# Both score products of a chunk as one group of 128 columns, and another order of L, mask and u

## What is computed

```python
attn = jnp.where(mask_incl, 0.0, -(kbc @ jnp.swapaxes(kc, -1, -2)))
for i in range(1, chunk):
    row = attn[..., i, :]
    upd = jnp.einsum('bhnj,bhnjk->bhnk', row, attn[..., :i])
    attn = attn.at[..., i, :i].add(upd)
attn = attn + jnp.eye(chunk, dtype=attn.dtype)
u = attn @ vc
w = attn @ kbc
def step(S, xs):
    q_i, k_i, u_i, w_i = xs
    attn_local = jnp.where(mask_strict, 0.0, q_i @ jnp.swapaxes(k_i, -1, -2))
    u_new = u_i - w_i @ S
    o_i = q_i @ S + attn_local @ u_new
    S = S + jnp.swapaxes(k_i, -1, -2) @ u_new
    return (S, o_i)
```

## Time and profile before

| | |
|---|---|
| median of 3 runs | 1094.88 us (1090.1 to 1096.59) |
| profiled execution | 1092.34 us, span 1090.6 us |
| busy over the span | PE 798.0 us, PE weight loads 495.7, DVE 743.3, ACT 454.5, POOL 201.5 |
| mean granted clock of TensorE | 0.856 |
| front stage | until about 622 us; rounds 0 to 15 start on DVE from 153.1 to 603.7 us |
| 390 to 450 us (60 us) | PE busy 57.74, DVE 56.02, ACT 33.08 |

### The profile page before, as it was taken

How to read it: one execution, slowest core, us unless ns; L and a number is a source line. 1 busy time by engine, 2 the same in 40 slices (tenths; PEclk the granted TensorE clock), 3 DMA queues, 4 the chain that set the end, 5 groups by cost and what they waited for, 6 DMA issues and landing times. The chain is left out here.

```text
span 1090.6 us, 40949 instructions
## 1 busy us (share of the span) xinstructions
PE 798.0 (73%) x18289; PEld 495.7 (45%) x18289; DVE 743.3 (68%) x1612; ACT 454.5 (42%) x864; POOL 201.5 (18%) x223
## 2 busy tenths in 40 slices
PE   2689859999898999988664575989877056666560
PEld 2244335555555555656664473545422034444440
DVE  4355988989899989989885149999995624222320
ACT  3497736556656655554110113566575111001000
POOL 2000000000000000000000000111111068887875
PEclk9999979999999999998766666989887579778775
DMA  3410111111110101101000092445452034444432
GB/s 102 83 40 26 36 36 33 45 40 38 38 38 23 38 28 38 38 28 38 14 14 13 27 295 80 112 108 125 106 131 54 20 98 84 71 82 74 72 37 24
DMA packets 86440, 66.13 MB, mean 61 GB/s; under 512 B 18504, under 2 KB 72952, under 8 KB 86264
## 3 DMA queue, kind: packets, MB, share of 16 engines
q1 hardware_dynamic: 72524, 53.90, 17.9%
q0 software_dynamic: 11264, 8.40, 5.8%
q10 hardware_dynamic: 2476, 1.22, 0.4%
HBM read 36.33 MB, written 27.15 MB: 58 GB/s over the span
## 5 line engine op out<-in xcount | busy, mean ns | idle before, releaser
L652 PE MATMUL ps_p<-hT,Wconv 128*128 128x512 f32 x384 | 191.8, 629 | 7.2 <-PEq L114 7.1
L750 DVE TENSOR_TENSOR f_L<-f_L,f_prod 128x60 f32<-128x60 f32 (+14 forms) x240 | 121.2, 505 | 8.3
L747 DVE TENSOR_TENSOR f_prod<-f_L 128x60 f32<-128x60 f32 (+14 forms) x240 | 118.7, 495 | 6.0
L652 PEld LDWEIGHTS ps_p<-hT,Wconv 128*128 128x128 f32 x384 | 70.3, 196 | 81.6 <-issue 75.5
L1365 POOL DMA_INDIRECT out_dram<-y,slot_row x64 | 101.2, 1582 | 28.3 <-issue 18.3
L1414 ACT ACTIVATE act_g<-pe_g 128x512 f32<-128x512 f32 x32 | 17.4, 594 | 167.4 <-PE pe_g L1392 141.0
L1382 PE MATMUL pe_x<-ident,got 128*128 128x128 f32 x64 | 15.8, 394 | 89.0 <-DMA got<-xh_dram,slot_row 89.0
L502 POOL COPY f_v_pad<-f_v_pad 128x32 f32<-128x32 f32 x15 | 4.4, 295 | 395.3 <-ACT f_v_pad L581 395.3
L1443 DVE SCALAR_TENSOR_TENSOR y<-pe_y,slot_w,gb_rows 128x128 f32<-128x128 f32 x64 | 18.0, 344 | 79.5 <-DMA out_dram<-y,slot_row 68.3
L1356 POOL DMA_INDIRECT got<-xh_dram,slot_row x64 | 62.1, 971 | 54.0 <-POOLq L1245 34.8
L632 PE MATMUL ps_a<-f_TT,f_r 32*32 32x64 f32 x2048 | 42.2, 250 | 34.0 <-DVE f_L L798 19.4
(11 more groups left out here) (256 smaller groups left out, 1808.7 us busy)
## 6 DMA issues: line engine op xcount, KB each, us to landing
w<-in_L_ffn_w_dram SPq DMA_DIRECT2D x48, 128.0 KB
s_tok_dram<-f_s_tok SPq DMA_DIRECT2D x16, 256.0 KB, 2.0
o_tok_dram<-f_o_tok SPq DMA_DIRECT2D x16, 256.0 KB, 2.0
b_s_in<-s_tok_dram SPq DMA_DIRECT2D x16, 256.0 KB, 2.9
b_o_in<-o_tok_dram SPq DMA_DIRECT2D x16, 256.0 KB, 3.1
b_x_in<-_attn_hidden_states_dram SPq DMA_DIRECT2D x64, 64.0 KB, 2.2
out_dram<-b_x SPq DMA_DIRECT2D x64, 64.0 KB, 1.8
xh_dram<-b_xh SPq DMA_DIRECT2D x64, 64.0 KB, 1.8
```

The costliest lines, as they stand in the source:

```text
L652: last = pe.matmul(ps[:, :], g.Wconv[:, which, tap, :], tokens(t, tap), start=(tap == 0), stop=(tap == TAPS - 1))
L747: dve.tensor_tensor(tmp, M[:, :, m + 1:, m:m + 1].broadcast_to([P, 2, rows, cols]), M[:, :, m:m + 1, 0:cols].broadcast_to([P, 2, rows, col ...
L750: dve.tensor_tensor(M[:, :, m + 1:, 0:cols], M[:, :, m + 1:, 0:cols], tmp, ALU.add).then_inc(s["solved"], 1)
```

## The change

The heads tile holds k and q heads side by side for each sequence, so that one matmul with 128 moving columns gives both scores of a pair of heads. They go into one tensor `ps_ab` over four banks; `ps_a` and `ps_b`, for u, o1 and o2, are its halves. As the scores now lie over both halves, their group waits for u and o of the round before, and u waits for the mask as well as for L. ACT's order stays, with `scores_ps` in the place of `ga_ps`.

```diff
-        heads_k, heads_q = k.sb("f_heads_k", [P, NB, G2, C]), k.sb("f_heads_q", [P, NB, G2, C])
+        heads = k.sb("f_heads", [P, NB, 2, G2, C])
+        heads_k, heads_q = heads[:, :, 0, :, :], heads[:, :, 1, :, :]
...
-        ps_a, ps_b = (stack.enter_context(nc.psum_tensor(n, [P, 2 * W], FP)) for n in ("ps_a", "ps_b"))
+        ps_ab = stack.enter_context(nc.psum_tensor("ps_ab", [P, 4 * W], FP))
+        ps_a, ps_b = ps_ab[:, 0:2 * W], ps_ab[:, 2 * W:4 * W]
+        scores = ps_ab[:, :].rearrange("p (b k g i) -> p b k g i", b=NB, k=2, g=G2)
...
                     need(pe, s["u_ready"], t3 - 4)
-                    per_pair(double(ps_a), narrow(k_cm[t3 % D_K]), lambda b, q: heads_k[quad(q), b, :, :].rearrange("p g c -> p (g c)"), every)\
-                        .then_inc(s["gl_ps"], 1)
+                    need(pe, s["attn_ready"], t3 - 1)
+                    need(pe, s["o_turned"], t3 - 4)
+                    per_pair(lambda b, q: ps_ab[quad(q), 2 * b * 64:2 * b * 64 + 2 * 64], narrow(k_cm[t3 % D_K]),
+                             lambda b, q: heads[quad(q), b, :, :, :].rearrange("p k g c -> p (k g c)"), every).then_inc(s["scores_ps"], 1)
                 if t is not None:
                     project(t, "k", 1, 1)
+                if t is not None:
+                    project(t, "v", 2, 0)
                 if d is not None:
                     need(pe, s["r_ready"], d)
                     need(pe, s["TT_ready"], d)
                     need(pe, s["L_taken"], min(d + 3, NCH - 1))
+                    need(pe, s["attn_ready"], min(d + 3, NCH - 1))
...
                 if t is not None:
-                    project(t, "v", 2, 0)
-                if t3 is not None:
-                    need(pe, s["attn_ready"], t3 - 1)
-                    need(pe, s["o_turned"], t3 - 4)
-                    per_pair(double(ps_b), narrow(k_cm[t3 % D_K]), lambda b, q: heads_q[quad(q), b, :, :].rearrange("p g c -> p (g c)"), every)\
-                        .then_inc(s["ga_ps"], 1)
-                if t is not None:
                     project(t, "v", 2, 1)
+                if t is not None:
+                    project(t, "q", 0, 0)
...
-                if t is not None:
-                    project(t, "q", 0, 0)
...
-                if t3 is not None:
-                    need(dve, s["gl_ps"], t3)
-                    need(dve, s["TT_ready"], t3 - 4)
-                    dve.transpose(L[t3 // 2 % 2][:, t3 % 2, :, :], ps_a[:, :].rearrange("p (n i) -> p i n", i=C)).then_inc(s["L_taken"], 1)
...
                     dve.transpose(kg_cm[t4 % D_KG][:, :], kg_tok[:, :]).then_inc(s["kg_ready"], 1)
+                if t3 is not None:
+                    need(dve, s["scores_ps"], t3)
+                    need(dve, s["TT_ready"], t3 - 4)
+                    dve.transpose(L[t3 // 2 % 2][:, t3 % 2, :, :].rearrange("p i (b g) -> p i b g", g=G2), scores[:, :, 0, :, :].rearrange("p b g i -> p i b g"))\
+                       .then_inc(s["L_taken"], 1)
+                    need(dve, s["o_ps"], t3 - D_A)
+                    dve.tensor_tensor(attn[t3 % D_A][:, :, :].rearrange("p (b g) i -> p b g i", g=G2), scores[:, :, 1, :, :],
+                                      g.causal[:, :].unsqueeze(1).unsqueeze(1).broadcast_to([P, NB, G2, C]), ALU.mult).then_inc(s["attn_ready"], 1)
+                part(0, 3)
                 if d is not None:
                     need(dve, s["u_ps"], d)
...
-                part(0, 3)
-                if t3 is not None:
-                    need(dve, s["ga_ps"], t3)
...
```

More of the change, by code:

```diff
@@ L410, in stage_front @@
                    nk_root nk_inv beta_ready bn_step gamma_ready kg_turned kg_ready w_ready heads_ready
-                   gl_ps ga_ps L_taken attn_ready L_masked solved TT_ready
+                   scores_ps L_taken attn_ready L_masked solved TT_ready
                    state_ready r_ps r_ready u_ps u_ready u_copied s_ps o1_ps o_ps o_turned o_copied fir_ready""".split()
@@ L549, in _ @@
                     need(act, s["k_ps"], t)
-                    need(act, s["ga_ps"], t - D_K)
+                    need(act, s["scores_ps"], t - D_K)
                     need(act, s["k_turned"], t - D_K)
@@ L567, in _ @@
                     t4 = i + 4
-                    need(act, s["ga_ps"], t4 - 1)
+                    need(act, s["scores_ps"], t4 - 1)
                     need(act, s["silu_q"], t4)
@@ L685, in _ @@
                 if t is not None:
-                    project(t, "v", 2, 0)
-                if t3 is not None:
-                    need(pe, s["attn_ready"], t3 - 1)
-                    need(pe, s["o_turned"], t3 - 4)
-                    per_pair(double(ps_b), narrow(k_cm[t3 % D_K]), lambda b, q: heads_q[quad(q), b, :, :].rearrange("p g c -> p (g c)"), every)\
-                        .then_inc(s["ga_ps"], 1)
+                    project(t, "v", 2, 1)
                 if t is not None:
-                    project(t, "v", 2, 1)
+                    project(t, "q", 0, 0)
                 if d is not None:
@@ L827, in _ @@
                     dve.transpose(u_wide[:, :].rearrange("p (b g z) -> p b g z", b=NB, g=G2), ps_a[:, :].rearrange("p (b i g) -> p b g i", b=NB, g=G2)).then_inc(s["u_ready"], 1)
-                part(0, 3)
-                if t3 is not None:
-                    need(dve, s["ga_ps"], t3)
-                    need(dve, s["o_ps"], t3 - D_A)
-                    dve.tensor_tensor(attn[t3 % D_A][:, :, :], ps_b[:, :].rearrange("p (n i) -> p n i", i=C),
-                                      g.causal[:, :].unsqueeze(1).broadcast_to([P, NI, C]), ALU.mult).then_inc(s["attn_ready"], 1)
                 part(3, 5)
```

## The result

The changed kernel takes 1114.39 us (median of 4 runs, 1112.63 to 1115.17), the kernel before, on the same chip, 1095.16 us: a ratio of 1.0182, with a 95% interval of 1.0146 to 1.0217. It is slower, by 1.5 to 2.2 per cent. The forecast was 1116 us with a range of 1100 to 1127. The profiled execution took 1113.67 us with a span of 1112.0, 21.4 more than before's.

What follows compares the result with a forecast made beforehand. DVE was taken to set the pace, with PE close behind. On the profiled 1092.3 us, +12.6, +6.8, +4.3, -5.0 and +3.6 gave +22.3, 1114.6; by the median 1117, stated as 1116, range 1100 to 1127.

Steps and rivals of the forecast that it cites:

- What bounds the kernel: Front-stage loop of 16 rounds: DVE sets the pace, PE is close behind and waits for DVE once per round.
- The wait for f_v_pad, +23.7: DVE's f_v_tok waits for ACT's later f_v_pad in rounds 0 to 10: 3.14, 2.28, 1.51 or 0.65 us each.
- The exchange of the mask's wait for u's in round 6, sum zero: DVE in round 6: f_attn's wait for the q scores is exchanged for an equal one before the u transpose.
- What is regained, -5.0: DVE waits behind PE's instruction stalls vanish in rounds 7, 10 and 11: 1.26, 2.49 and 1.25 us; bounds 0 and 6.6.
- The clock, +3.6: Spread matmuls of rounds 1, 3, 5 and 7: PE idle grows to 4.5 us, slower clock costs 0.90 us each.
- The matmuls, 0: PE's score groups: one of 128 columns costs 3.84 us, like two of 64; saved instructions are off DVE's path.
- The rival of PE's supply: Fewer PE loads and multiplies, 3.39 us a group, no stalls: faster, about 1082 us; decisive if f_v_tok waits are small; chance 0.06.
- The dearer rival's stalls: PE's s and o1 groups back to back: stalls like 1.83 us in rounds 7 to 10, +7.3; about 1127 us, chance 0.12.
- The sum: All terms over the loop: +22.3 us on the profiled execution of 1092.3, giving 1114.6; stated as 1116.
- a difference behind 625 us: Stretch after the loop, where nothing is edited: a difference there would show the prediction wrong.

Runs made afterwards that it cites:

- e1: The changed kernel with DVE's f_v_tok transpose moved behind five more update steps, part(5, 10): 1087.25 us, ratio to the kernel before 0.9923.
- e6: The changed kernel with ACT's f_v_pad moved ahead of its four copies into f_heads, DVE's order kept: 1093.18 us, ratio to the kernel before 0.9997.
- e2: The changed kernel with PE's s group back ahead of the first half of q: 1116.24 us, ratio to the kernel before 1.0191.
- e7: The kernel before with DVE's u transpose behind the first three update steps only in rounds 11 to 15: 1089.3 us, ratio 0.9955.
- e5: The changed kernel with the merged score group issued as two of 64 columns, same place and banks: 1128.61 us, ratio to the kernel before 1.0351.
- e8: e3 with the merged score group issued as two of 64 columns: 1102.21 us, ratio to the kernel before 1.0084.
- e3: The changed kernel with the edits of both e1 and e2: 1085.17 us, ratio to the kernel before 0.9893.
- e4: The kernel before, 64-column groups kept, with DVE's u transpose behind the first three update steps: 1099.2 us, ratio 1.0045.

## Why the prediction was right, and where it was not

*What bounds the kernel.* Right while projections run; in rounds 12 to 15 of the kernel before DVE waits for PE, 3.8 to 10.1 us at a time. DVE's queue sets the pace: e1 and e6 take 22.8 and 20.5 us of DVE's wait away and get 27 and 21 us back; e2 takes 14 us of PE's stalls away and gets nothing.

*The wait for f_v_pad, +23.7.* Right, the core of the forecast. It came 11 times for 22.8 us: 3.02 or 3.03 in each of rounds 0, 2, 4 and 6 (3.14 forecast), 2.15 or 2.16 in 1, 3 and 5 (2.28), 1.50 and 1.49 in 8 and 10 (1.51), 0.62 in 7 and 9 (0.65). The method is to carry over: add up the other engine's chain from the operation that moves to the one that is read, subtract the way of the waiting engine between the same two points. ACT's chain was 5.2 + 1.3 = 6.5 us in round 6.

*The exchange of the mask's wait for u's in round 6, sum zero.* Nearly: u waited 1.37 us there instead of 0.72, 0.48 or 0.49 in rounds 2, 4, 8 and 10, and 2.02 in round 0.

*What is regained, -5.0.* The number came out in rounds 7 to 11, in part by luck: the 1.26, the 1.25 and the 2.49 are gone, the 1.64 became 0.48, and rounds 7 to 11 give -0.3 us where the terms made +4.3 - 5.0 + 0.9 = +0.2. But the two waits of round 10 are gone in e7 too, without any edit there, so that these 2.49 us come from the new order is not shown. The failed step is that I stopped at round 11. Rounds 12 and 13 had waits of 3.95 and 3.76 us for u, larger than all I counted, and the three update steps moved ahead of u fill them. The changed kernel gives back 5.5 us in rounds 12 to 14, and e7, which does nothing else, 5.0 in rounds 11 to 14. The forecast followed the rounds in which f_v_pad is late and left out those in which the new order helps. The waits of 3.76 and 3.85 in rounds 14 and 15 stay (3.76 and 4.01), as no update step is left to put ahead of them.

*The clock, +3.6.* The mechanism was right, the term mis-sized. Spreads of rounds 3 and 7 in the changed kernel:

```profile
259.51 2.05 PE L669 MATMUL ps_p<-f_dense,spread 128*128 128x512 f32 x2 [4.19 <-ACT f_dense L627]
...
400.77 1.10 PE L669 MATMUL ps_p<-f_dense,spread 128*128 128x512 f32 x2 [0.85 <-ACT f_dense L627]
```

and of rounds 2 and 6 in the kernel before:

```profile
218.80 1.62 PE L666 MATMUL ps_p<-f_dense,spread 128*128 128x512 f32 x2 [2.50 <-ACT f_dense L624]
...
349.29 2.04 PE L666 MATMUL ps_p<-f_dense,spread 128*128 128x512 f32 x2 [3.14 <-ACT f_dense L624]
```

Four spreads run at half clock (2.04 or 2.05 us), and round 1's takes 1.39. But the kernel before already had 2.00, 2.04 and 1.62, and over rounds 1 to 7 the spreads sum to 11.78 us against 10.06: +1.7. The idle times ahead were not 4.5 us in rounds 1, 3, 5 and 7, but 2.96, 4.19, 3.02 and 0.85. PE's new stalls in the q·state group had used up part of them: in e2, without these stalls, the same idle times are 4.52, 5.55, 4.31 and 4.10, and the seven spreads sum to 13.9 us, 3.9 over before, where the forecast had 3.6.

*The matmuls, 0.* Here two errors about cancelled. "One group of 128 costs 2 x 1.92 = 3.84 us: nothing is saved" is nearly right as a duration (3.63 measured), and "the saved instructions are also not on DVE's path" is wrong. The comparison that counts is with two groups at the new place, and e5 puts it at 14 us. I also charged nothing for bringing the groups to one place and for letting f_L wait for both. In the kernel before, projections stood between them and DVE took f_L after the first. With the new order and unmerged groups (e8) the kernel is 0.8% slower than before, with merged ones (e3) 1.1% faster. What bringing the groups together costs by itself no run shows, since e8 also has DVE's other moves. A total near 0 fits the measured loop; that both parts are 0 does not.

*The rival of PE's supply* named the right mechanism (fewer loads and multiplies, fewer stalls), at 0.06 and decisive only if DVE's waits were small. That condition is what e3 meets, and there it comes out: 1085, though not by the price of 3.39 us a group that it was given. The Trainium skill's fixed cost per matmul ("TensorEngine Tiling (Array Packing)", "Instruction Overhead") has the same sign, but the saving is not of that kind: without a stall the split groups take 3.78 us and the merged one 3.69.

*The dearer rival's stalls* came (21.2 us in the q·state group), early rounds as well as late, and cost nothing beside DVE's wait, as e2 shows.

*The sum.* The loop lost 13.8 us from the first f_r to the last, where the terms said 22.3. In rounds 0 to 6 it is 19.5 us against 22.1, in rounds 7 to 11 -0.3 against +0.2, in rounds 12 to 14 -5.5 against nothing. The spacing of f_r in rounds 0 to 6 was 33.8 to 36.5 us, where I said 35 to 36. Yet the profiled execution ended 21.4 us later, and the medians differ by 19.2. Most of the rest lies behind the loop, in code that is word for word the same. From the last f_r to the first gather of the expert stage it is 269.2 us in the trace of before and 275.9 after; the eight experiments have 272.0 to 277.3, e7 and e4 with before's own back stage 274.2 and 274.7. So before's profiled execution was short there, and since e4 and e7 have neither the merge nor its order on PE, it does not look like the change's doing; its cause stays open. The prediction had named a difference behind 625 us as a sign of being wrong, and by that sign it was wrong here. That the forecast of 1116 us lies so near the measured 1114.4 is luck in the size: 8.5 us too much in the loop, 7.6 us outside it that no term foresaw. The direction and the main term are not luck.

## What to carry to other kernels

When an operation on the pacing engine moves later, follow its results through the other engines and back: a reader on the same engine may now find the round trip longer than its own work in between, and one reader moved behind work that needs nothing (e1) was worth 27 us. Look also at the rounds in which the pipeline drains, since a wait with no work ahead of it there is where a later place gains (e7). And price a merge of small matmuls against the same work unmerged at the new place, not by its columns alone: here the stalls decided. No run has the merged group with the u transpose left where it was, so the best order for the merge is open.

## What the hardware showed that was not expected

Stalls of PE that the profile puts down to "issue" sit in long stretches of small matmuls with a weight load each, and go when the stretch is broken. 256 matmul instructions of 64 columns at one place: 14 stalls of 1.0 to 2.1 us in 16 groups. The same columns in 128 instructions: none. The s and q·state groups back to back: 21.2 us of stalls, 17.1 of them in rounds 0 to 10; with one projection of 1.99 us between them 7.2, of which 0.8 in these rounds; in the later ones no projection is left to stand between them.

The traces also show what ends these stalls. Queue 8 carries instructions in packets of 16 KB, in the kernel before and in the changed one:

```profile
q8 instruction: 144, 2.36, 0.9%
...
q8 instruction: 128, 2.10, 0.8%
```

The 4096 loads and multiplies that the merge saves are 16 packets, so a packet is 256 of PE's instructions. Over the ten traces, from 150 to 620 us, PE has 264 waits of 0.2 us or more put down to "issue", and every one ends 1.1 to 1.7 us behind the end of such a packet; of times picked at random 11 to 14 per cent lie there. In round 6 of the changed kernel the packet ends at 385.96 us and PE goes on at 387.35. No two packets start less than 3.2 us apart in any trace. A group of 64 columns uses up 256 instructions in 1.92 us, the merged group in 3.63. So the stalls fit waits for the next instructions. That the merged group is just slow enough to be supplied is an estimate from these numbers: 3.2 us is the least distance seen, not a measured limit.
